# A list scheduler with its own lengths for each group of images, and spare products on TensorE

## The chip, the cores and the metric

The kernel runs on one core of one Trainium2 chip. The metric is the time on the device in microseconds (us) of one execution, lower being better. Its engines work side by side: TensorE (PE, matrix products), VectorE (DVE), ScalarE (ACT), GpSimd (POOL), and SyncE (SP), which only issues DMA transfers here.

## The reference

The network is one vision block on 32 images of 96 x 96 pixels, 36 patches of an image being its tokens (1152 tokens, 192 features):

```
h = patches(x) @ W.T + b                       # 768 -> 192
h = h + mamba(layernorm(h))                    # in-projection and gate (192 -> 384), a selective scan
                                               # over the 36 tokens with 16 states, out-projection, FFN of 512
h = h + moe(layernorm(h))                      # router, 16 experts (192 -> 2 x 192 -> 192), top 4 of 16
```

In the scan each of 384 channels has 16 states: `h[t] = a_bar[t] * h[t-1] + dt*z*B[t]`, and `y[t] = sum over states of h[t] * C[t]`. The step size `dt` is a softplus of a projection. The experts are computed for all tokens and weighted with the router's result. Everything is float32.

## The kernel before, in words

The images are cut into five groups, called cuts, of 4, 7, 7, 7 and 7 images (144 and 252 tokens). For each cut the work is a long list of steps, each a few instructions, and each step has a part on one or two engines:

- *Before the scan*: six embed parts, mean, variance, `roots` (VectorE) and `power` (GpSimd) for the norm, `spread` (TensorE puts the root on all partitions), `scale` (VectorE), three in-projections with gate, a projection to the inputs of the scan (`xproj`, `dt_in`, `bc_copy`), `delta` with its copies on ScalarE (`delta_abs`), the softplus as a product of factors (`factor`, `poly`, `log1p`), and `drive` (on VectorE in cut 0, on GpSimd in the others).
- *C spreads*: eight times `c_spread` (TensorE) and `c_copy` (ScalarE) put C on all partitions. In the kernel the first `c_spread` of a cut waits for `bc_low` and for the copies of `delta` (lines 861 to 871).
- *Scan*: 24 steps of `decay` (ScalarE), `fill` (TensorE), `drive_b` and `advance` (VectorE, the recurrence), `read` (GpSimd) and `collect` (TensorE).
- *After the scan*: out-projection, norm, the FFN (`ffn_up`, `ffn_tanh`, `ffn_product`, `down`), and the next norm.
- *Experts*: the router (`x_logits`, `x_topk`, `x_exp`, `x_route`, `x_turn`, `x_mix`), `x_start`, then 24 units of `x_gate`, `x_linear`, work on VectorE, ScalarE and GpSimd, and `x_down`. `x_start` opens the sums in the PSUM bank `sums`.
- *Splitting* the first expert weights in two parts, `split_w1`, sixteen steps on ScalarE and GpSimd with loads from DRAM, once at the start.

All engines follow one order, written by `schedule()` (line 234) before the program is built: `run` (line 610) lets each engine go through this order and issue what is its own. Semaphores see to correctness, so the order settles only which work stands before which on each engine.

`schedule()` is a list scheduler on the host. It holds five streams: the steps before the scan with the C spreads of cuts 0, 2, 3 and 4; those of cut 1; the scans; the work after the scans; the experts; with `split_w1` as a further one. A stream is a list of turns (a turn is one to a few steps), and each turn has a place, in units of scan steps, at which it is due. Again and again it takes, of the turns at the streams' heads whose needs are met, the one with the lowest

```
score = place + WAIT_WEIGHT * waits
```

`waits` is the time for which TensorE and VectorE would stand idle for this turn. `lay` (line 250) works it out: it lays the turn's steps on the engines' own times, with durations from the table `COST` (line 341) scaled as `0.25 + 0.75 * size` where size is the cut's tokens over 252. A step starts when its engine is free and its inputs are ready. For scan and expert steps the inputs are listed (`rests_on`, line 220); for every other step they are the ends of the steps before it in its turn, and for a turn's first step the end of the stream's turn before. So the planner starts a cut's first `c_spread` after its `drive`.

Of the kernel before, what the change touches and what calls it, by code (L numbers as in the profile page):

```python
# [20 lines left out]
P = 128  # L21
# [23 lines left out]
NC = len(CUTS)  # L45
# [188 lines left out]
def schedule():  # L234

    out, given, ended = [], set(), {}  # L240
    free = {"P": 4.0, "V": 4.0, "S": 10.0, "G": 4.0}
    streams, reading = [], [0.0]

    def stream(turns, places):
        streams.append(list(zip(turns, places)))

    def spread_over(n, first, last):
        return [first + (last - first) * k / max(1, n - 1) for k in range(n)]

    def lay(turn, chain, keep):  # L250

        at, waits, end, pool_from = dict(free), 0.0, {}, reading[0]
        for c, step, i in turn:
            size = TOKENS[c] / TM
            ready = chain
            found = rests_on(c, step, i)
            if found is not None:
                ready = max([end.get((c, *f), ended.get((c, *f), 0.0)) for f in found])
            elif end:
                ready = max(ready, max(end.values()))  # L260
            for engine, us in COST[step]:
                start = max(at[engine], ready)
                if step in TWO_PORTS and pool_from <= start:
                    start = max(start, at["G"])
                if engine in "PV":
                    waits += start - at[engine]
                elif engine == "G":
                    pool_from = start
                at[engine] = start + us * (0.25 + 0.75 * size)
                ready = at[engine] + LATENCY[engine]  # L270
            end[(c, step, i)] = ready
        if keep:
            free.update(at)
            reading[0] = pool_from
            ended.update(end)
        return waits, max(end.values())

    prep = []
    for c in range(NC):
        b, s = of_cut(c, before_scan()), of_cut(c, c_turns())  # L280
        if c == 0:
            places = spread_over(len(b), -24.0, -1.0) + spread_over(len(s), -1.0, 5.0)
        elif c == 1:
            places = spread_over(len(b), -16.0, 20.0) + spread_over(len(s), 17.0, 24.0)
        else:
            p = SCAN_STEPS * (c - 1)
            places = spread_over(len(b), p, p + BEFORE_SPAN) + spread_over(len(s), p + 17.0, p + 24.0)
        if c == 1:
            stream(b + s, places)
        else:  # L290
            prep += list(zip(b + s, places))
    streams.append(prep)
    scans = []
    for c in range(NC):
        turns = scan_turns(c)
        if c:
            ends = of_cut(c - 1, scan_end(c - 1))
            turns = of_cut(c, turns)
            first = turns.index([(c, "collect", 0)])
            turns = turns[:first - 2] + ends + turns[first - 2:]  # L300
        else:
            turns = of_cut(0, turns)
        scans += list(zip(turns, spread_over(len(turns), SCAN_STEPS * c, SCAN_STEPS * (c + 1) - 0.4)))
    scans += [(turn, SCAN_STEPS * NC) for turn in of_cut(NC - 1, scan_end(NC - 1))]
    streams.append(scans)
    posts, routed = [], []
    for c in range(NC):
        a, x = of_cut(c, after_scan()), of_cut(c, expert_turns())
        p = SCAN_STEPS * (c + 1) + 2.0
        q = p + (AFTER_SPAN if c + 2 < NC else LAST_AFTER_SPAN)  # L310
        posts += list(zip(a, spread_over(len(a), p, q)))
        routed += list(zip(x, spread_over(len(x), q + 0.5, q + (EXPERT_SPAN if c + 2 < NC else LAST_EXPERT_SPAN))))
    streams += [posts, routed]
    stream([[(0, "split_w1", n)] for n in range(2 * PAIRS)], [-12.0, -8.0, -5.0, -2.0] + spread_over(12, *SPLIT_SPAN))
    chain = [0.0] * len(streams)

    while any(streams):
        best = None
        for n, turns in enumerate(streams):
            if not turns:  # L320
                continue
            turn, place = turns[0]
            inside = {s for s in turn}
            if any(f not in given and f not in inside for step in turn for f in needed(*step)):
                continue
            waits, end = lay(turn, chain[n], False)
            score = place + WAIT_WEIGHT * waits
            if best is None or score < best[0]:
                best = (score, n)
        assert best, [t[0] for t in streams if t]  # L330
        n = best[1]
        turn, _ = streams[n].pop(0)
        _, end = lay(turn, chain[n], True)
        chain[n] = end
        out += turn
        given.update(turn)
    return out
# [2 lines left out]

COST = {
    "embed": (("P", .87),), "embedded": (("S", .9),), "mean": (("P", .85),), "center": (("V", .6),),
    "square": (("S", .56),), "variance": (("P", .9),), "roots": (("V", .18),), "power": (("G", 1.),),
    "spread": (("P", .45),), "scale": (("V", 1.5),), "inproj": (("P", 1.7),),
    "gate": (("S", .32),), "z": (("V", .38),), "xproj": (("P", 1.27),), "dt_in": (("S", .45),),
    "bc_copy": (("V", .36),), "bc_high": (("S", .36),), "bc_low": (("V", .4),), "delta": (("P", .65),),
    "delta_abs": (("S", 1.2),), "delta_exp": (("S", .75),), "factor": (("S", .9),),
    "poly": (("V", .7),), "log1p": (("V", .72),), "drive": (("G", 2.2),), "c_spread": (("P", .25),),
    "c_copy": (("S", .52),), "decay": (("S", .82),), "fill": (("P", .25),), "drive_b": (("V", .6),),
    "advance": (("V", 1.13),), "read": (("G", 1.2),), "collect": (("P", .85),), "y": (("V", .43),),  # L350
    "outproj": (("P", 1.27),), "y1_add": (("V", .6),), "square2": (("S", .62),), "variance2": (("P", .9),),
    "roots2": (("V", .18),), "power2": (("G", 1.),), "spread2": (("P", .23),),
    "scale2": (("V", .78),), "ffn_up": (("P", 1.7),), "ffn_tanh": (("S", .36),), "ffn_product": (("V", .78),),
    "down": (("P", 1.7),), "h1": (("V", .55), ("G", 1.25)), "mean3": (("P", .85),), "center3": (("V", .58),),
    "square3": (("S", .62),), "variance3": (("P", .9),), "roots3": (("V", .18),), "power3": (("G", 1.),),
    "spread3": (("P", .45),), "scale3": (("V", 1.5), ("G", 1.3)),
    "t_high": (("S", .62),), "t_low": (("G", 1.25),), "x_logits": (("P", .9),), "x_topk": (("V", 2.2),),
    "x_exp": (("S", .3),), "x_route": (("V", 1.2),), "x_turn": (("P", .25),), "x_mix": (("S", .7),),
    "x_start": (("P", .85),), "x_gate": (("P", .6),), "x_linear": (("P", .6),), "x_min": (("V", .43),),
    "x_tanh": (("S", .33),), "x_one": (("S", .4),), "x_low": (("V", .41),), "x_gated": (("V", .34),),  # L360
    "x_glu": (("G", .68),), "x_scale": (("G", .68),), "x_down": (("P", .47),), "x_finish": (("V", 1.2),),
    "split_w1": (("S", 1.), ("G", 2.)),
}

TWO_PORTS = {"x_gated", "poly", "log1p", "bc_low"}

LATENCY = {"P": 0.22, "V": 0.12, "S": 0.1, "G": 0.14}
WAIT_WEIGHT = 0.5
BEFORE_SPAN = 15.5
AFTER_SPAN, LAST_AFTER_SPAN = 20.9, 22.0  # L370
EXPERT_SPAN, LAST_EXPERT_SPAN = 25.1, 21.7
SPLIT_SPAN = (2.0, 36.0)


def vit_tower(nc, patches, embed_w, in_w, in_w_rest, xproj_w, dt_w, out_w, ffn_w, ffn_w_rest,
# [5 lines left out]
    with ExitStack() as ctx:  # L381
# [10 lines left out]
        w_embed = sb("w_embed", [P, KP, 2 * P])  # L392
# [14 lines left out]
        decay = sb("decay", [P, NJ, STATES])  # L407
# [8 lines left out]
        at, first = {}, 0  # L416
# [13 lines left out]
        us = sb("us", [P, 2, NJ, TM])  # L430
# [9 lines left out]
        dt_in = sb("dt_in", [DT_RANK, TM])  # L440
# [326 lines left out]
        def _(pe):  # L767
            def mm(out, lhsT, rhs, start, stop, shared=False, turned=False):

                return nc.tensor.matmul(out, lhsT, rhs, start=start, stop=stop, skip_group_check=shared,  # L770
                                        is_transpose=turned)

            def embed(c, part):
# [236 lines left out]
            def x_down(c, n):  # L1010
# [9 lines left out]
                else:  # L1020
# [5 lines left out]
            run({"embed": embed, "mean": mean, "variance": variance, "spread": spread, "inproj": inproj,  # L1026
                 "xproj": xproj, "delta": delta, "c_spread": c_spread, "fill": fill, "collect": collect,
                 "outproj": outproj, "variance2": variance2, "spread2": spread2, "ffn_up": ffn_up, "down": down,
                 "mean3": mean3, "variance3": variance3, "spread3": spread3, "x_logits": x_logits,
# [578 lines left out]
```

## Time and profile before

| what | value |
|---|---|
| median of 3 runs | 625.59 us (624.6 to 626.37) |
| the profiled execution | 627.44 us, span 625.6 us |
| mean granted clock of TensorE | 0.945 |
| TensorE, weight loads busy | 557.0 us, 479.1 us |
| VectorE, GpSimd, ScalarE busy | 475.5 us, 388.3 us, 295.2 us |

The span goes from the first to the last instruction; the execution's own time lies around it. Busy time is per engine, and engines overlap. The granted clock is TensorE's own: 1.0 is 2.4 GHz and 0.5 is 1.2 GHz, and these are its only two levels in the records, so a mean between them is a mixture in time. Nearly all TensorE instructions have one line, 770, that of the helper `mm`; they are told apart by their tiles: `pre` and `post` are PSUM banks of the work before and after the scan (cut 1 is prepared in `post`), `fills` and `y_sum` those of the scan, `gate_up`, `linear_up` and `sums` those of the experts.

### The profile page before, as it was taken

Reading aid. Unit: us, or ns where it says so; the run is one execution under the profiler, and the core shown is the slowest. Engines: PE = TensorE matmul, PEld = TensorE weight load, DVE = VectorE, ACT = ScalarE, POOL = GpSimd, SP = SyncE. Lnnn points to the kernel's source line nnn. Section 1 sums busy time; section 2 is a strip of 40 time slices with the busy share of each in tenths; the row PEclk is TensorE's granted clock in tenths of the full one; section 3 lists DMA queues with packets and bytes.
Section 4 is the critical chain, followed back from the end, with each engine's and each line's share of the span. In section 5 each row is a group of like instructions: output and inputs, shape, how many; then the busy total and the mean of one; then the engine's idle time right before and its main releaser. Section 6 shows DMA issues by size and latency. Waiting matters only on the chain.

```text
span 625.6 us, 10398 instructions
## 1 busy us (share of the span) xinstructions
PE 557.0 (89%) x3361; PEld 479.1 (77%) x3361; DVE 475.5 (76%) x897; ACT 295.2 (47%) x699; POOL 388.3 (62%) x447
## 2 busy tenths in 40 slices
PE   3959589977899999989999997999998889978896
PEld 3748478866698988879887885988886768857785
DVE  1166868889789789979879996999989556565664
ACT  1167846483544475544446474445442324323442
POOL 3257777767456458857555984767677355564674
PEclk9779959989899999999999997999999889997999
DMA  9993533432053343413343341554342266553781
GB/s 238 308 299 97 164 119 90 189 135 92 1 155 100 106 155 95 162 33 112 111 171 112 105 141 46 135 157 143 121 177 88 50 207 213 178 174 104 238 274 52
DMA packets 41827, 88.34 MB, mean 141 GB/s; under 512 B 9581, under 2 KB 34477, under 8 KB 35501
## 3 DMA queue, kind: packets, MB, share of 16 engines
q1 hardware_dynamic: 41772, 87.68, 43.4%
q8 instruction: 26, 0.43, 0.3%
q14 instruction: 29, 0.23, 0.1%
HBM read 77.24 MB, written 10.40 MB: 140 GB/s over the span
## 4 chain that ended last, share of the span: by engine, by line
PE 61%; DVE 15%; issue 6%; DMA 6%; ACT 5%; POOL 4%; SPq 2%; POOLq 0%; DVEq 0%; ACTq 0%
PE post L770 12%; PE y_sum L770 10%; PE sums L770 10%; PE gate_up L770 10%; PE pre L770 8%; PE linear_up L770 8%; DVE state L1255 4%; DMA w<-w_store 3%; PE fills L770 3%; DVE fills L1246 2%; DVE dts L1222 2%; SPq L709 1%; POOL read L1456 1%; DMA hid<-patches 1%; DVE scratch L1354 1%
## 5 line engine op out<-in xcount | busy, mean ns | idle before, releaser
L1456 POOL TENSOR_TENSOR read<-state,c_all 128x504 f32<-128x504 f32 (+1 forms) x120 | 147.0, 1228 | 83.2 <-DVE state L1255 54.8
L1255 DVE TENSOR_TENSOR_SCAN state<-a_bar,fills 128x504 f32<-128x504 f32 (+1 forms) x120 | 133.0, 1109 | 12.1 <-ACT a_bar L1035 4.1
L1485 POOL TENSOR_TENSOR scratch<-scratch 128x252 f32<-128x252 f32 (+1 forms) x120 | 81.6, 680 | 87.4 <-DVE scratch L1369 82.4
L770 PE MATMUL y_sum<-read,ident 128*128 128x252 f32 (+1 forms) x480 | 122.5, 382 | 4.1 <-POOL read L1456 3.7
L1035 ACT ACTIVATE scratch<-scratch 128x252 f32<-128x252 f32 (+1 forms) x120 | 47.3, 394 | 147.0 <-DVE scratch L1354 146.8
L770 PE MATMUL sums<-hid,w 128*128 128x252 f32 (+1 forms) x480 | 103.8, 377 | 4.8 <-POOL hid L1494 4.8
L770 PE MATMUL gate_up<-t_high,w 128*128 128x252 f32 (+1 forms) x360 | 89.3, 318 | 14.5 <-DVE route L1332 7.2
L770 PEld LDWEIGHTS y_sum<-read,ident 128*128 128x128 f32 x480 | 86.3, 201 | 19.8 <-issue 7.1
L1035 ACT ACTIVATE a_bar<-dts,decay 128x245 f32<-128x245 f32 (+1 forms) x240 | 100.2, 470 | 2.2 <-DVE dts L1230 2.2
L1494 POOL TENSOR_TENSOR hid<-scratch,route_rows 128x252 f32<-128x252 f32 (+1 forms) x120 | 84.9, 708 | 14.4 <-DMA route_rows<-mix_rows 7.6
L770 PE MATMUL linear_up<-t_high,w 128*128 128x252 f32 (+1 forms) x360 | 85.8, 308 | 2.3 <-ACT mix_w L1035 1.7
L770 PEld LDWEIGHTS gate_up<-t_high,w 128*128 128x128 f32 x360 | 64.3, 193 | 27.8 <-issue 17.0
L1354 DVE TENSOR_SCALAR scratch<-gate_up,vec 128x252 f32<-128x252 f32 (+1 forms) x120 | 54.0, 450 | 40.0 <-PE gate_up L770 39.1
L1246 DVE TENSOR_TENSOR fills<-us,fills 128x504 f32<-128x504 f32 (+1 forms) x120 | 75.6, 630 | 7.8 <-PE fills L770 7.6
L1369 DVE SCALAR_TENSOR_TENSOR scratch<-scratch 128x252 f32<-128x252 f32 (+1 forms) x120 | 76.1, 634 | 4.4 <-POOL scratch L1485 0.3
L1361 DVE TENSOR_SCALAR scratch<-linear_up,vec 128x252 f32<-128x252 f32 (+1 forms) x120 | 54.2, 451 | 22.1 <-PE linear_up L770 19.1
L770 PEld LDWEIGHTS linear_up<-t_high,w 128*128 128x128 f32 x360 | 63.8, 193 | 6.6 <-ACT mix_w L1035 2.7
L770 PE MATMUL fills<-bc_parts,pick_state 128*128 128x252 f32 (+1 forms) x240 | 60.6, 336 | 8.0 <-DVE state L1255 8.0
L770 PE MATMUL gate_up<-t_low,w 128*128 128x252 f32 (+1 forms) x240 | 62.0, 282 | 0.0
L770 PE MATMUL linear_up<-t_low,w 128*128 128x252 f32 (+1 forms) x240 | 61.8, 281 | 0.0
L770 PEld LDWEIGHTS sums<-hid,w 128*128 128x128 f32 x480 | 49.0, 163 | 15.9 <-POOL hid L1494 6.6
L1035 ACT ACTIVATE scratch<-scratch,ones 128x252 f32<-128x252 f32 (+1 forms) x120 | 58.5, 488 | 4.3 <-POOL scratch L1485 0.5
(166 smaller groups left out, 851.9 us busy)
## 6 DMA issues: line engine op xcount, KB each, us to landing
w<-w_store SPq DMA_DIRECT2D x40, 1152.0 KB, 5.7
route_rows<-mix_rows SPq DMA_DIRECT2D x192, 63.0 KB, 3.0
w_store<-w SPq DMA_DIRECT2D x8, 1152.0 KB, 5.0
scratch<-expert_w SPq DMA_DIRECT2D x16, 384.0 KB, 5.6
w<-expert_w SPq DMA_DIRECT2D x1, 2304.0 KB
route_rows<-mix_rows SPq DMA_DIRECT2D x48, 36.0 KB, 2.8
w_embed<-embed_w SPq DMA_DIRECT2D x3, 256.0 KB, 3.9
x_patch<-patches SPq DMA_DIRECT2D x1, 756.0 KB, 5.0
```

Of the source, the lines that this page charges most:

```text
L709: sp.dma_start(route_rows[part * REST:(part + 1) * REST, slot, 0:tok(c)], mix_rows[c % 2][e:e + 1, 0:tok(c)].to_broadcast([REST, tok(c)]))\
L770: return nc.tensor.matmul(out, lhsT, rhs, start=start, stop=stop, skip_group_check=shared, is_transpose=turned)
L1035: return nc.scalar.activation(out, in_, func, **kw)
L1222: dve.scalar_tensor_tensor(dt, factors[:, k % FACTOR_SLOTS, :, 0:tok(c)], LOG1P[k][1], dt if k else sp_exp[:, :, 0:tok(c)], ALU.add, ALU.m ...
L1246: dve.tensor_tensor(b_x, twice(us[:, c % 2, j, 0:tok(c)]), b_x, ALU.mult).then_inc(bx_ready.sem, 1)
L1255: dve.tensor_tensor_scan(pair(state, i, c), pair(a_bar, i, c), pair(fills, i, c), 0.0, ALU.mult, ALU.add).then_inc(scanned.sem, 1)
L1354: dve.tensor_scalar(g_min[un % 2][:, 0:tok(c)], half(gate_up, c, 0), col("b1_gate", un), LIMIT, ALU.add, ALU.min).then_inc(gate_min.sem, 1)
L1361: dve.tensor_scalar(l_min[:, 0:tok(c)], half(linear_up, c, 0), col("b1_linear", un), 1.0 + LIMIT, ALU.add, ALU.min).then_inc(linear_min.se ...
L1369: dve.scalar_tensor_tensor(product[un % 2][:, 0:tok(c)], l_min[:, 0:tok(c)], 1.0 - LIMIT, g_min[un % 2][:, 0:tok(c)], ALU.max, ALU.mult).t ...
L1456: pool.tensor_tensor(by_state(pair(read, i, c)), by_state(pair(state, i, c)), c_all[:, n:n + 2, 0:tok(c)], ALU.mult).then_inc(read_out.sem, 1)
L1485: pool.tensor_tensor(glu[:, 0:tok(c)], product[un % 2][:, 0:tok(c)], g_one[un % 2][:, 0:tok(c)], ALU.mult)\
L1494: pool.tensor_tensor(hid[:, un % HID_TILES, 0:tok(c)], glu[:, 0:tok(c)], route_rows[:, slot, 0:tok(c)], ALU.mult).then_inc(hid_ready.sem, 1)
```

## The change

Two things change, both in `schedule()`, and one helper is added on TensorE.

The planner's numbers: some durations in `COST`, mostly of ScalarE, are set anew; the fixed share of a step's duration is now its engine's own (`FIXED`) instead of 0.25; `WAIT_WEIGHT` goes from 0.5 to 1.5; the lengths over which the places of a group are spread are given for each cut and stream (for cuts 0 and 1 those of `BEFORE_SPANS` are not read, as their places are given elsewhere).

Spare products: `lay` also notes the longest idle time of TensorE within the turn (`idle`). Before a turn with 0.8 us or more of it, as long as the first `x_start` hasn't been given, the order gets `(idle - 0.2) / 0.24` steps `warm`, and ten more stand before cut 1's first embed part. A `warm` step multiplies a 128 x 128 tile of the embed weights with itself into the bank `sums`, waits for nothing and signals nothing; its result is never read.

```
     def lay(turn, chain, keep):
...
+                if engine == "P":
+                    idle[0] = max(idle[0], start - at["P"])
...
-                at[engine] = start + us * (0.25 + 0.75 * size)
+                at[engine] = start + us * (FIXED[engine] + (1.0 - FIXED[engine]) * size)
...
-            places = spread_over(len(b), p, p + BEFORE_SPAN) + spread_over(len(s), p + 17.0, p + 24.0)
+            places = spread_over(len(b), p, p + BEFORE_SPANS[c]) + spread_over(len(s), p + 17.0, p + 24.0)
...
-        q = p + (AFTER_SPAN if c + 2 < NC else LAST_AFTER_SPAN)
+        q = p + AFTER_SPANS[c]
...
-        routed += list(zip(x, spread_over(len(x), q + 0.5, q + (EXPERT_SPAN if c + 2 < NC else LAST_EXPERT_SPAN))))
+        routed += list(zip(x, spread_over(len(x), q + 0.5, q + EXPERT_SPANS[c])))
...
+        if (0, "x_start", 0) not in given and idle[0] >= WARM_FROM:
+            out += [(0, "warm", k) for k in range(int((idle[0] - WARM_MARGIN) / WARM_STEP))]
+        out += [(0, "warm", k) for k in range(WARM_AT.get(turn[0], 0))]
         out += turn
...
-    "poly": (("V", .7),), "log1p": (("V", .72),),
+    "poly": (("V", 0.9),), "log1p": (("V", 0.85),),
...
+FIXED = {"P": 0.08, "V": 0.22, "S": 0.5, "G": 0.22}
-WAIT_WEIGHT = 0.5
-BEFORE_SPAN = 15.5
-AFTER_SPAN, LAST_AFTER_SPAN = 20.9, 22.0
-EXPERT_SPAN, LAST_EXPERT_SPAN = 25.1, 21.7
+WAIT_WEIGHT = 1.5
+BEFORE_SPANS = (39.85, 11.8, 19.57, 15.32, 14.59)
+AFTER_SPANS = (23.32, 20.9, 19.43, 21.5, 24.02)
+EXPERT_SPANS = (22.68, 25.68, 25.23, 23.04, 21.62)
+WARM_FROM, WARM_MARGIN, WARM_STEP = 0.8, 0.2, 0.24
+WARM_AT = {(1, "embed", 0): 10}
...
+            def warm(_, k):
+                mm(sums[:, 0:P], w_embed[:, 0, 0:P], w_embed[:, 0, 0:P], True, True)
```

Besides `poly` and `log1p`, fourteen other durations move by 0.01 to 0.06 us.

## Rows read from the trace of the kernel before

**Rows 1.** The page: TensorE's busy time, and its granted clock in 40 slices (tenths)
```profile
PE 557.0 (89%) x3361; PEld 479.1 (77%) x3361; DVE 475.5 (76%) x897; ACT 295.2 (47%) x699; POOL 388.3 (62%) x447
...
PEclk9779959989899999999999997999999889997999
```

**Rows 2.** The page: the chain that ended last, by engine
```profile
PE 61%; DVE 15%; issue 6%; DMA 6%; ACT 5%; POOL 4%; SPq 2%; POOLq 0%; DVEq 0%; ACTq 0%
```

**Rows 3.** Windows by stage: length; busy PE, PEld, DVE, ACT, POOL; clock; DMA share, GB/s
```profile
0.00:170.00 170.00, 130.44 (x680) 112.06 (x681) 114.27 (x197) 92.49 (x229) 103.05 (x112) 0.87 0.49 159
170.00:480.00 310.00, 300.37 (x1888) 262.98 (x1888) 274.38 (x493) 152.75 (x360) 206.86 (x232) 0.99 0.38 122
480.00:625.60 145.60, 126.15 (x796) 104.03 (x794) 86.88 (x208) 49.95 (x110) 78.39 (x104) 0.94 0.50 161
```

**Rows 4.** Windows at low clock
```profile
14.70:24.40 9.70, 8.77 (x33) 7.52 (x34) 1.23 (x5) 0.00 (x0) 3.24 (x4) 0.50 1.08 335
...
76.00:93.00 17.00, 13.94 (x52) 12.20 (x52) 11.94 (x18) 8.82 (x22) 14.11 (x15) 0.50 0.37 116
...
380.00:390.00 10.00, 6.52 (x26) 5.57 (x27) 7.09 (x22) 5.27 (x14) 4.31 (x4) 0.66 0.04 10
```

**Rows 5.** Timeline, 15 to 26 us: start, length, engine, line, what, [idle before <-releaser]
```profile
15.63 2.05 PE L770 MATMUL post<-hid,w_embed 128*128 128x252 f32 x4 [3.33 <-DMA hid<-patches]
...
17.48 0.33 PE L770 MATMUL pre<-mean_ones,squares 128*72 128x1 f32 x2
...
18.39 2.03 PE L770 MATMUL post<-hid,w_embed 128*128 128x252 f32 x4
...
18.88 1.04 POOL L1406 TENSOR_TENSOR roots<-roots,minus_half 72x4 f32<-72x4 f32 x1 [3.10 <-DVE roots L1186]
...
20.21 0.69 PE L770 MATMUL pre<-ident,roots 72*128 72x72 f32 x4
...
21.58 0.36 DVE L1196 SCALAR_TENSOR_TENSOR squares<-centered,vec,pre 128x144 f32<-128x144 f32 x1
...
22.46 0.69 PE L770 MATMUL pre<-squares,w_in 128*128 128x144 f32 x2
...
24.38 1.21 PE L770 MATMUL post<-hid,w_embed 128*128 128x252 f32 x4
...
25.43 0.41 PE L770 MATMUL pre<-squares,w_in 128*128 128x144 f32 x2
...
25.67 0.41 PE L770 MATMUL pre<-squares,w_in_rest 128*128 128x144 f32 x2
```

**Rows 6.** Timeline of TensorE: the first and the longest of its early waits
```profile
11.46 0.48 PE L770 MATMUL pre<-h0s,mean_ones 128*128 128x144 f32 x2 [2.20 <-ACT h0s L1035]
...
41.30 1.10 PE L770 MATMUL post<-ident,roots 126*128 126x126 f32 x4 [4.91 <-POOL roots L1406]
```

**Rows 7.** Timeline: the drives (us<-dts) and first C spreads (bc_parts,pick_state), cuts 0, 1
```profile
41.80 0.61 DVE L1237 TENSOR_TENSOR us<-dts,zs 128x432 f32<-128x432 f32 x1
...
42.05 0.68 PE L770 MATMUL pre<-bc_parts,pick_state 128*128 128x144 f32 x2
...
82.84 0.80 PE L770 MATMUL post<-bc_parts,pick_state 128*128 128x252 f32 x2
...
85.48 1.78 POOL L1444 TENSOR_TENSOR us<-dts,zs 128x756 f32<-128x756 f32 x1
```

**Rows 8.** The chain in order of time: start, length, what
```profile
44.32 3.74 PE post L770 x8
...
77.02 1.33 PE y_sum L770 x4
...
87.44 0.81 PE post L770 x2
...
139.35 1.83 DVE dts L1222
...
164.48 3.48 PE pre L770 x8
```

More of the change, by code:

```diff
@@ L241, in schedule @@
     free = {"P": 4.0, "V": 4.0, "S": 10.0, "G": 4.0}
-    streams, reading = [], [0.0]
+    streams, reading, idle = [], [0.0], [0.0]
     def stream(turns, places):
@@ L252, in lay @@
         at, waits, end, pool_from = dict(free), 0.0, {}, reading[0]
+        idle[0] = 0.0
         for c, step, i in turn:
@@ L342 @@
     "embed": (("P", .87),), "embedded": (("S", .9),), "mean": (("P", .85),), "center": (("V", .6),),
-    "square": (("S", .56),), "variance": (("P", .9),), "roots": (("V", .18),), "power": (("G", 1.),),
+    "square": (("S", 0.61),), "variance": (("P", .9),), "roots": (("V", .18),), "power": (("G", 1.),),
     "spread": (("P", .45),), "scale": (("V", 1.5),), "inproj": (("P", 1.7),),
-    "gate": (("S", .32),), "z": (("V", .38),), "xproj": (("P", 1.27),), "dt_in": (("S", .45),),
+    "gate": (("S", 0.37),), "z": (("V", .38),), "xproj": (("P", 1.27),), "dt_in": (("S", .45),),
     "bc_copy": (("V", .36),), "bc_high": (("S", .36),), "bc_low": (("V", .4),), "delta": (("P", .65),),
     "delta_abs": (("S", 1.2),), "delta_exp": (("S", .75),), "factor": (("S", .9),),
[L348 to L351, printed above, removed]
+    "poly": (("V", 0.9),), "log1p": (("V", 0.85),), "drive": (("G", 2.2),), "c_spread": (("P", .25),),
+    "c_copy": (("S", 0.57),), "decay": (("S", 0.8),), "fill": (("P", .25),), "drive_b": (("V", 0.62),),
+    "advance": (("V", 1.15),), "read": (("G", 1.26),), "collect": (("P", .85),), "y": (("V", .43),),
+    "outproj": (("P", 1.27),), "y1_add": (("V", .6),), "square2": (("S", 0.62),), "variance2": (("P", .9),),
     "roots2": (("V", .18),), "power2": (("G", 1.),), "spread2": (("P", .23),),
-    "scale2": (("V", .78),), "ffn_up": (("P", 1.7),), "ffn_tanh": (("S", .36),), "ffn_product": (("V", .78),),
+    "scale2": (("V", .78),), "ffn_up": (("P", 1.7),), "ffn_tanh": (("S", 0.37),), "ffn_product": (("V", .78),),
     "down": (("P", 1.7),), "h1": (("V", .55), ("G", 1.25)), "mean3": (("P", .85),), "center3": (("V", .58),),
@@ L358 @@
     "x_exp": (("S", .3),), "x_route": (("V", 1.2),), "x_turn": (("P", .25),), "x_mix": (("S", .7),),
-    "x_start": (("P", .85),), "x_gate": (("P", .6),), "x_linear": (("P", .6),), "x_min": (("V", .43),),
-    "x_tanh": (("S", .33),), "x_one": (("S", .4),), "x_low": (("V", .41),), "x_gated": (("V", .34),),
-    "x_glu": (("G", .68),), "x_scale": (("G", .68),), "x_down": (("P", .47),), "x_finish": (("V", 1.2),),
+    "x_start": (("P", .85),), "x_gate": (("P", .6),), "x_linear": (("P", .6),), "x_min": (("V", 0.44),),
+    "x_tanh": (("S", 0.38),), "x_one": (("S", 0.45),), "x_low": (("V", 0.43),), "x_gated": (("V", .34),),
+    "x_glu": (("G", 0.7),), "x_scale": (("G", 0.71),), "x_down": (("P", .47),), "x_finish": (("V", 1.2),),
     "split_w1": (("S", 1.), ("G", 2.)),
@@ L1024, in x_down @@
                     last.then_inc(pe_hid.sem, 1)
-            run({"embed": embed, "mean": mean, "variance": variance, "spread": spread, "inproj": inproj,
+            run({"warm": warm, "embed": embed, "mean": mean, "variance": variance, "spread": spread, "inproj": inproj,
                  "xproj": xproj, "delta": delta, "c_spread": c_spread, "fill": fill, "collect": collect,
```

## The prediction

> **What bounds the kernel now.** I read the busy times first. TensorE is the busiest engine: 557 us of a 625.6 us span, and the row of granted clock under it is far from flat [rows 1]. Next I read the chain that ended last: 61% of it is TensorE, 15% VectorE, 4% GpSimd [rows 2]. Then I cut the span by stage. From 170 to 480 us TensorE is busy for 300.4 of 310 us at a mean clock of 0.99, so there it is simply full. Before 170 us it is busy for 130.4 of 170 us at a mean clock of 0.87: both idle and slow. After 480 us it is busy for 126.2 of 145.6 us at 0.94 [rows 3].
>
> A mean clock of 0.87 over 170 us, with only the two levels 1.0 and 0.5, is 2 x 0.13 x 170 = 44 us at half speed. They come in blocks: 14.7 to 24.4 us, and 76 to 93 us, where TensorE was busy for 13.9 of 17 us at half clock [rows 4]; between them one near 38 to 48 us, and short ones near 138 and 165 us. Each follows a stretch in which TensorE had stood still: the first comes after the wait of 3.33 us for the patches of cut 1 [rows 5].
>
> A block costs only what of it lies on the path, so it has to be walked. In the first, the path is on TensorE from 15.63 us: an embed part (to 17.48), the variance (to 18.39), a root on VectorE and GpSimd (to 19.92), the spread (from 20.21, since an embed part stood before it), the scale on VectorE (to 21.94), the first in-projection (22.46 to 24.38) [rows 5].
>
> **The change, part by part.** The time is summed against the profiled execution, 627.44 us with a span of 625.6; it lies 0.3% above the median of 625.59, so I take the difference from 625.6.
>
> *What a spare tile costs.* It is one 128 x 128 by 128-column product in f32, two matmul instructions. The same with 144 columns takes 25.67 - 25.43 = 0.245 us at full clock and 0.48 us at half (four of them from 22.46 to 24.38) [rows 5]. By columns, 128/144 of it: 0.22 us, or 0.43 at half clock. Tiles wait for nothing, so they start when TensorE's queue reaches them. They are free as long as the wait that follows is longer than they are, and otherwise the rest delays every matmul behind them.
>
> *How many.* The ten before cut 1's first embed part take 2.2 us, inside its 3.33 us wait for a transfer that they can't lengthen [rows 5]. For the others the planner's own idle time decides. Twelve waits of at least 0.8 us stand in the trace before the first expert start, 25 us together; the first is 2.20 us, the longest 4.91 us [rows 6]. At (wait - 0.2)/0.24 each, without the transfer that the planner doesn't see, they ask for about 75 tiles. The planner sees two more that the kernel doesn't have. It lets the first C spread of a cut begin when its stream's last turn, the drive, has ended. In the trace cut 0's C spread starts at 42.05 us while the drive runs to 42.41, and cut 1's at 82.84 us, 2.6 us before its drive even begins [rows 7]. It listens only to the projection's copies. If the planner sees 2 to 5 us there, each spread gets 8 to 20 tiles that no real wait covers: 1.8 to 4.4 us each. So 100 to 130 tiles in all, 22 to 29 us of TensorE time, against 39.6 us of idle TensorE before 170 us [rows 3].
>
> *What a kept clock gives back.* First block: the embed part 0.93, the variance 0.45, the spread's delay behind an embed part 0.29 and its own half 0.24, the in-projection's delay 0.52 and half 0.96: 3.4 us [rows 5]. Second block: 3.74 us of in-projection on the chain at 44.32 us, half of it 1.9 us. Third block: ten TensorE pieces of the chain between 77.02 and 88.25 us add up to 8.6 us; half is 4.3 us, but VectorE and GpSimd are busy for 11.9 and 14.1 of these 17 us [rows 4] and come next, so it is between 0 and 4.3 and I take 3. Near 139 us the chain is on VectorE, so the down-projection's slowness gives nothing. At 164.48 us 3.48 us of embed on the chain give 1.7 us [rows 8]. Sum: 3.4 + 1.9 + 3 + 0 + 1.7 = 10 us.
>
> *What misplaced tiles take.* The two C spreads, 3.6 to 8.8 us together. Behind the one at 42 us stand cut 1's in-projection and the third fill of the scan, behind the one at 82 us the copies of C and the last fills of cut 0. VectorE has work of its own at both places, so part of it is covered: I take 3.5 us. Were the clock low there all the same, a tile would be 0.43 us and the two would take up to 17 us. Tiles elsewhere may overrun by a few tenths; I leave them in the range.
>
> *The new order.* Tripling the weight of a wait makes the planner prefer a turn that starts at once on TensorE or VectorE to one that is due. The per-engine fixed shares shorten cut 0's TensorE steps and lengthen its ScalarE ones, since only cut 0 is shorter; the spans move turns by a few scan steps (those of cuts 0 and 1 in the list for the steps before the scan are read nowhere, as both cuts have places of their own). No instruction is added by this. TensorE has 9.6 us of idle time from 170 to 480 us [rows 3], and one slow place in it, 380 to 390 us, with 6.5 us busy at a clock of 0.66 [rows 4]; the planner itself can't win more than these 12 us there. A bad order can lose as much: a recurrence pushed back holds the fills. Between -12 and +12 I take 0, since the stage is 97% full already. The waits after 480 us belong to the last cuts, which have little to put between, and get no tiles.
>
> The Trainium skill ("TensorE: Matmul & The Clock Gate", Part 1, on the two states) says the ramp penalty is under 1% of a typical kernel's span. By that the whole clock gain would be an estimate of under 6.3 us and, with my misplaced tiles, the change under 3 us. The rows speak against it here: 44 us at half clock before 170 us, in five blocks and not one ramp.
>
> Sum: -10 + 3.5 + 0 = -6.5 us. After 170 us TensorE is full, so what is won before it moves the end by the same. 625.6 - 6.5 = **619.1 us**, 1.0% less.
>
> **Rivals.**
>
> *More comes back* (602 to 614 us). The misplaced tiles lie beside VectorE's work, all of the third block returns (10 + 1.3 = 11.3 us), and the new order wins a few of the 12 us. For it: TensorE is only 77% busy before 170 us. Against it: ScalarE, VectorE and GpSimd bound the third block. At the middle: 610.
>
> *The tiles don't hold the clock, or what they win is lost at once* (623.7 to 627.5 us). The planner places by its own times; where a real wait outlasts the tiles, as at 41.30 us, the clock may fall behind them. Then they lie in idle time and change nothing. For it: planned and real waits differ by transfers and by GpSimd's splitting of the weights. Against it: it has to fail in all of the first three blocks.
>
> *Misplaced tiles decide* (slower). Mechanism: the C spreads' wait exists in the planner alone. If both get 20 tiles and the clock there is low, it takes 17 us against 10 - 3 = 7 us from what other blocks give back: +10, 636 us. At full clock and without the third block it takes 8.8 against 7: +1.8, 627.4 us. It decides from 32 such tiles at full clock, or 16 at half. For it: both spreads start in the trace without the planned wait. Against it: the heavier weight on waits makes the planner put other turns there first, and fewer tiles follow.
>
> *The order alone loses* (slower, about 630 us). The scan's turns are passed over for turns that start at once, VectorE's recurrences come late, and half of the 12 us in the full stage goes on top of a small early gain. Nothing in the trace tells its sign.
>
> **How the numbers follow.** About 0.3% (1.9 us) is what a measurement can tell from no change here. Chances: forecast (614 to 623.7) 0.44, more comes back 0.20, nothing 0.13, misplaced tiles 0.12, order 0.11. Faster is the first two, 0.64; same 0.13; slower 0.23. The forecast's own range is 614 to 623.7; leaving a tenth out at each end gives 606 to 631.
>
> **What would show it.** Right: granted clock near 1.0 from 14 to 24 us, cut 0's first in-projection ending near 21 us instead of 24.4, and the first expert start some 6 us earlier, with all later stages moved by the same. The misplaced tiles show as a run of some ten spare products directly before the first C spread of cuts 0 and 1, with VectorE or ScalarE waiting for it. The prediction is wrong if the early stage gains over 10 us, if it gains nothing with the clock high, or if 170 to 480 us changes its length by over 5 us: then the order, not the tiles, made the difference.

## The result: 2.45% slower

The changed kernel takes 641.18 us (median of 4 runs, 638.82 to 642.47), the one before 625.98 us on the same chip. The ratio is 1.0245, 95% interval 1.0214 to 1.0276: 15 us slower, where 6.5 us less were forecast and the range ended at 631.

The page of the changed kernel: TensorE's busy time and its granted clock in 40 slices, and the chain that ended last.

```profile
PE 579.6 (91%) x3655; PEld 505.5 (79%) x3655; DVE 470.8 (74%) x897; ACT 295.3 (46%) x699; POOL 388.7 (61%) x447
...
PEclk9899999799999999989999997999999799998899
...
PE 63%; DVE 9%; DMA 8%; POOL 7%; issue 6%; ACT 4%; SPq 3%; POOLq 0%; DVEq 0%; ACTq 0%
```

147 spare products were placed, some 34 us at 0.23 us each; TensorE's busy time grows by only 22.6 us [rows 1]: its other products take less time, as more of them run at the full clock. On the chain VectorE's share falls from 15% to 9%, DMA's rises from 6% to 8% and GpSimd's from 4% to 7% [rows 2].

The stages of the changed kernel (length; busy TensorE, weight loads, VectorE, ScalarE, GpSimd; clock; DMA share, GB/s):

```profile
0.00:170.00 170.00, 143.94 (x941) 131.90 (x941) 107.70 (x176) 88.73 (x218) 100.10 (x109) 0.96 0.48 159
170.00:480.00 310.00, 298.39 (x1874) 261.96 (x1873) 267.18 (x502) 154.24 (x366) 202.67 (x228) 0.98 0.37 118
480.00:639.70 159.70, 137.24 (x844) 111.68 (x842) 95.92 (x221) 52.30 (x116) 85.90 (x112) 0.94 0.47 155
```

The clock of the first 170 us is 0.96 where it was 0.87 [rows 3]: over the stage the tiles do what they are for. In its first block they do so only in part, 0.82 where it was 0.50 [rows 4]:

```profile
14.70:24.40 9.70, 5.92 (x28) 5.17 (x29) 0.22 (x2) 2.36 (x6) 4.88 (x6) 0.82 0.42 129
```

But VectorE gets 107.7 us of work done in that stage instead of 114.3. So the clock was kept for the most part and the work fell behind all the same. A few marks, read from the timelines of the profiled executions (us from the start), show where:

| mark | before | changed | difference |
|---|---|---|---|
| step sizes of cut 0 (`log1p` starts) | 41.2 | 44.2 | +3.0 |
| step sizes of cut 1 | 84.0 | 81.3 | -2.7 |
| step sizes of cut 2 | 141.3 | 157.8 | +16.5 |
| first expert start, cut 0 | 173.2 | 186.8 | +13.6 |
| result of cut 0 | 264.9 | 272.6 | +7.7 |
| result of cut 2 | 479.4 | 487.2 | +7.8 |
| expert start, cut 3 | 490.9 | 504.5 | +13.6 |
| result of cut 4 | 622.0 | 636.0 | +14.0 |

Two places stand out. In the first 170 us the kernel falls behind; 13.6 us are missing at the first expert start, and 7.8 of them still at cut 2's result. And the 11.5 us between cut 2's result and cut 3's expert start have become 17.2.

**The first place.** Timeline of ScalarE and TensorE in the changed kernel (start, length, engine, line, what, [idle before <-releaser]):

```profile
12.21 2.40 PE L784 MATMUL sums<-w_embed 128*128 128x128 f32 x20
...
15.86 1.98 ACT L1053 ACTIVATE w<-scratch 128x384 fp32r<-128x384 f32 x4 [4.47 <-DMA scratch<-expert_w]
...
17.75 0.43 ACT L1053 ACTIVATE squares<-centered 128x288 f32<-128x288 f32 x1
...
18.08 0.25 ACT L1053 ACTIVATE read<-post 48x128 f32<-48x128 f32 x1
...
18.48 3.62 PE L784 MATMUL post<-hid,w_embed 128*128 128x252 f32 x8 [3.87 <-ACT read L1053]
...
22.61 0.23 PE L784 MATMUL pre<-mean_ones,squares 128*72 128x1 f32 x2
...
26.48 0.48 PE L784 MATMUL pre<-squares,w_in 128*128 128x144 f32 x2 [0.25 <-DVE squares L1214]
```

The tiles end at 14.6 us and the patches of cut 1 were there near 15.6 us in the kernel before [rows 5]. But the first embed part now waits for ScalarE's `read` (the exponential of the decay, which the kernel wants done before it writes the bank `post`), and that stands behind two steps of `split_w1`, which wait 4.47 us for raw expert weights to arrive. In the kernel before, ScalarE squared at 12.82 us and split at 24.82:

```profile
12.82 0.44 ACT L1035 ACTIVATE squares<-centered 128x288 f32<-128x288 f32 x1 [1.50 <-DVE centered L1178]
...
24.82 0.93 ACT L1035 ACTIVATE w<-scratch 128x384 fp32r<-128x384 f32 x2
```

The variance of cut 0 moves from 17.48 to 22.61 us and its first in-projection from 22.46 to 26.48. The Trainium skill ("TensorE: Matmul & The Clock Gate", Part 1, "Architectural detail") calls ScalarE's queue strictly first in, first out; the trace agrees: the square's input was ready at 12.9 us, when VectorE's centering ended, and the square starts at 17.75 us, behind the splits.

It happens again with cut 2:

```profile
115.73 0.94 ACT L1053 ACTIVATE w<-scratch 128x384 fp32r<-128x384 f32 x2 [4.32 <-DMA scratch<-expert_w]
```

```profile
117.23 0.38 PE L784 MATMUL pre<-mean_ones,squares 128*126 128x1 f32 x2 [3.59 <-ACT squares L1053]
...
118.75 2.03 PE L784 MATMUL y_sum<-read,ident 128*128 128x252 f32 x4
```

ScalarE waits 4.32 us for raw weights, cut 2's variance on TensorE waits 3.59 us for the square behind it, and the next products run at half clock (2.03 us for four that take 1.01 at full clock).

**The second place.** TensorE of the changed kernel after cut 2's result:

```profile
493.78 0.76 PE L784 MATMUL gate_up<-t_high,w 128*128 128x252 f32 x2 [3.17 <-DVE route L1350]
...
494.98 1.89 PE L784 MATMUL y_sum<-read,ident 128*128 128x252 f32 x4
497.53 5.38 PE L784 MATMUL post<-y,w_out 128*128 128x252 f32 x12 [0.66 <-DVE y L1278]
502.70 0.62 PE L984 MATMUL linear_up<-ident,route 126*16 126x126 f32 x2
...
504.47 1.01 PE L784 MATMUL sums<-mix_w,b 128*128 128x252 f32 x4
```

TensorE waits 3.17 us for the router of cut 3, comes back at half clock, and does the whole out-projection of cut 4 (5.38 us) before the router's transpose, on which the expert start depends. In the order before, half of the out-projection stood there and half behind:

```profile
484.81 0.47 PE L770 MATMUL gate_up<-t_high,w 128*128 128x252 f32 x2 [1.98 <-DVE route L1332]
...
485.47 2.62 PE L770 MATMUL post<-y,w_out 128*128 128x252 f32 x6
487.88 0.63 PE L966 MATMUL linear_up<-ident,route 126*16 126x126 f32 x2
...
489.66 1.44 PE L770 MATMUL post<-y,w_out 128*128 128x252 f32 x6
490.93 1.01 PE L770 MATMUL sums<-mix_w,b 128*128 128x252 f32 x4
```

**The misplaced tiles.** Of the 147 tiles 32 stand before C spreads: 15 before the first of cut 0, 12 before the first of cut 2, none before the first of cut 1. Both of these runs are on the chain of the changed kernel (here without the part of each that runs under other work):

```profile
45.02 3.35 PE sums L784 x30
...
157.99 2.79 PE sums L784 x24
```

### The profile page after: what moved, and what is told of

Its sections match the earlier page's. It is cut to its first block, busy times and chain, and to the rows that moved or that the text cites. A ratio compares the mean times of both kernels' runs of the same rounds, so it can differ in the third digit from the quotient of the medians.

```text
span 639.7 us, 10986 instructions
## 1 busy us (share of the span) xinstructions
PE 579.6 (91%) x3655; PEld 505.5 (79%) x3655; DVE 470.8 (74%) x897; ACT 295.3 (46%) x699; POOL 388.7 (61%) x447
## 4 chain that ended last, share of the span: by engine, by line
PE 63%; DVE 9%; DMA 8%; POOL 7%; issue 6%; ACT 4%; SPq 3%; POOLq 0%; DVEq 0%; ACTq 0%
PE post L784 13%; PE y_sum L784 11%; PE sums L784 11%; PE gate_up L784 9%; PE pre L784 9%; PE linear_up L784 7%; DMA w<-w_store 3%; DMA scratch<-expert_w 3%; PE fills L784 3%; DVE state L1273 2%; POOL read L1474 2%; POOL hid L1512 1%; DVE fills L1264 1%; SPq L723 1%; POOL scratch L1503 1%
## 5 line engine op out<-in xcount | busy, mean ns | idle before, releaser
L1474 POOL TENSOR_TENSOR read<-state,c_all 128x504 f32<-128x504 f32 (+1 forms) x120 | 144.9, 1212 | 83.4 <-DVE state L1273 52.1
L1503 POOL TENSOR_TENSOR scratch<-scratch 128x252 f32<-128x252 f32 (+1 forms) x120 | 83.7, 698 | 89.5 <-DVE scratch L1387 80.2
L1387 DVE SCALAR_TENSOR_TENSOR scratch<-scratch 128x252 f32<-128x252 f32 (+1 forms) x120 | 68.7, 573 | 4.2
L784 PEld LDWEIGHTS sums<-hid,w 128*128 128x128 f32 x480 | 49.0, 163 | 15.6 <-POOL hid L1512 6.2
```

The source lines that it names most:

```text
L1387: dve.scalar_tensor_tensor(product[un % 2][:, 0:tok(c)], l_min[:, 0:tok(c)], 1.0 - LIMIT, g_min[un % 2][:, 0:tok(c)], ALU.max, ALU.mult).t ...
L1474: pool.tensor_tensor(by_state(pair(read, i, c)), by_state(pair(state, i, c)), c_all[:, n:n + 2, 0:tok(c)], ALU.mult).then_inc(read_out.sem, 1)
L1503: pool.tensor_tensor(glu[:, 0:tok(c)], product[un % 2][:, 0:tok(c)], g_one[un % 2][:, 0:tok(c)], ALU.mult)\
```

## Experiments

Ratios are against the kernel before, run beside each. Where a difference of two versions is given, it is the difference of their ratios, times 626 us; by the two intervals it is known to 2 to 3 us either way (an estimate).

**Without tiles (`no_tiles`).**
```
-            out += [(0, "warm", k) for k in range(int((idle[0] - WARM_MARGIN) / WARM_STEP))]
+            pass
-WARM_AT = {(1, "embed", 0): 10}
+WARM_AT = {}
```


> The changed kernel without its spare products (all 147 left out), same order otherwise. Theory W (the new order makes ScalarE wait for the raw expert weights, and that costs the 14 us): the time stays above 635 us, and with a low clock in the first 50 us it may reach 645. Rival T (the spare products stand in TensorE's way): 622 to 630 us.

644.76 us, 1.0292 (1.0251 to 1.0333). The order alone costs 18 us. The tiles give 3 of them back by the difference (1.0292 against 1.0245), but the two intervals overlap, so that gain is not clear of noise. That the tiles are what loses is out for the new order.

**Tiles alone (`before_tiles`).** The old planner, with the rule for spare products and `warm` as the only addition.

> The kernel before with the spare products alone: its old planner, numbers and order, and 148 tiles put in by the new rule. Theory W: the tiles by themselves are no loss, 615 to 627 us. Rival T: they alone bring most of the loss, 633 to 642 us.

632.51 us, 1.0098 (1.0068 to 1.0127): between the two. With the old order the tiles lose 6.1 us. TensorE of this run around the two C spreads:

```profile
40.01 0.65 PE L779 MATMUL post<-ident,roots 126*128 126x126 f32 x4 [3.45 <-POOL roots L1418]
40.49 4.70 PE L779 MATMUL sums<-w_embed 128*128 128x128 f32 x26
44.94 0.42 PE L779 MATMUL pre<-bc_parts,pick_state 128*128 128x144 f32 x2
```

```profile
83.35 4.18 PE L779 MATMUL sums<-w_embed 128*128 128x128 f32 x36
87.29 0.48 PE L779 MATMUL post<-bc_parts,pick_state 128*128 128x252 f32 x2
```

4.7 and 4.2 us of tiles stand before the first C spreads of cuts 0 and 1, with no idle time behind either, and both are on this run's chain. In the kernel before, these C spreads came at 42.05 and 82.84 us [rows 7]; here they come at 44.94 and 87.29.

**Splits held back (`pinned`).** Each split may be placed only after the step that it followed in the order before (the fourteenth: after cut 2's square). The planner then also lays some other steps a few places earlier or later, so this run changes more than the splits.
```
+    if step == "split_w1" and i in SPLIT_AFTER:
+        return [SPLIT_AFTER[i]]
...
+SPLIT_AFTER = {0: (0, 'gate', 0), 1: (1, 'embedded', 0), 2: (0, 'bc_high', 0), ...
```


> The changed kernel, with each of the 16 steps that split the raw expert weights held back in the planner until the step that it followed in the order before (for the fourteenth: until cut 2's square). Theory W: the waits of ScalarE for raw weights near 16, 39 and 116 us go, cut 0's variance comes near 17 us again instead of 22.6, and the time falls by 8 to 14 us, to 626 to 632. Rival T, or a rival O (the later order of scans and experts loses the time): no more than 3 us come back, 636 to 642.

637.15 us, 1.0178 (1.0153 to 1.0202). 4 us come back, half or less of what theory W asked for. Its step sizes of cut 0 start at 38.3 us and its cut 2 result at 479.6, level with before (479.4); the 17 us up to cut 3's expert start remain, and so does a later end.

**Two splits early, nothing else (`before_split_early`).**
```
+    early = [(0, "split_w1", 0), (0, "split_w1", 1)]
+    out = [step for step in out if step not in early]
+    at_center = out.index((0, "center", 0))
+    return out[:at_center] + early + out[at_center:]
```


> The kernel before, with only the first two steps that split the raw expert weights moved ahead of cut 0's centering and square, as in the changed kernel; no tiles. Theory W: cut 0's variance moves from 17.5 to about 22.5 us and the whole kernel is 3 to 5 us longer, 629 to 631. Rivals T and O: what cut 0 loses there is covered by the waits behind it, within 1.5 us of 625.6.

630.04 us, 1.0067 (1.0042 to 1.0093): 4.2 us, the price of the early splits by themselves, as theory W had it. Every other step keeps its place in this run. ScalarE's wait and what stands behind it are those of the changed kernel:

```profile
16.49 1.99 ACT L1038 ACTIVATE w<-scratch 128x384 fp32r<-128x384 f32 x4 [5.48 <-DMA scratch<-expert_w]
...
18.72 0.26 ACT L1038 ACTIVATE read<-post 48x128 f32<-48x128 f32 x1
...
20.93 0.33 PE L773 MATMUL pre<-mean_ones,squares 128*72 128x1 f32 x2
...
25.92 0.69 PE L773 MATMUL pre<-squares,w_in 128*128 128x144 f32 x2
```

Two steps of 1 us each, moved forward by 8 and 14 us (from 24.82 and 31.19 us) on a queue of an engine that is busy for half of the time, cost 4 us at the end.

**Tiles alone, none before C spreads (`tiles_no_spread`).**
```
-        if (0, "x_start", 0) not in given and idle[0] >= WARM_FROM:
+        if (0, "x_start", 0) not in given and idle[0] >= WARM_FROM and turn[0][1] != "c_spread":
```


> The kernel before with the spare products alone, without the 35 of them that stand before C spreads (113 stay). Theory M (the tiles that cost are those before C spreads, where only the planner waits): 4 to 8 us less than with all 148, so 624 to 628. Rival A (every tile costs, by lying in front of work whose real wait differs from the planned one): the loss falls with the number only, 35/148 of 6.6 us, to 630 to 632.

623.99 us, 0.9960 (0.9934 to 0.9986): the misplaced tiles (those before C spreads) are what loses in the old order. These 35 tiles before C spreads cost 8.6 us in the old order; the other 113 gain 2.5. This version beats both kernels, by a little. Its chain shows why the gain is small:

```profile
14.76 1.12 PE post L779 x4
...
19.42 1.22 PE pre L779 x8
...
26.78 7.54 DMA scratch<-expert_w
34.34 0.94 ACT w L1047 x2
```

Cut 0's first in-projection starts at 19.42 us instead of 22.46 [rows 5], 3.0 us earlier; 0.9 of that is the patches of cut 1, on which the embed part waits in both and which came at 14.76 instead of 15.63 us. Then a load of raw weights, 7.54 us, lets ScalarE's next split start only at 34.34 us, after 1.70 us of idle time, and cut 0's step sizes come at 39.02 instead of 41.16. SyncE issues that load behind TensorE's last embed part of cut 1, so a faster TensorE does move its start, here and before:

```profile
26.78 1.71 SPq L685 DMA_DIRECT2D scratch<-expert_w x1
```

```profile
30.81 0.65 SPq L676 DMA_DIRECT2D scratch<-expert_w x1
```

What it doesn't shorten is the load itself. Issued 4.0 us earlier, the load took 7.54 us; in the kernel before it had landed when ScalarE came to it at 36.50 us, 5.7 us after its issue.

**The planner's numbers one by one (`weight15`, `spans`, `durations`).** Each time the kernel before with only `WAIT_WEIGHT = 1.5`; or only the new lists of spans; or only the new `FIXED`; no tiles. The run `durations` leaves the table `COST` as it was, though its expectation speaks of new durations, so no run has the new `COST` as its only change; and in that table `poly` and `log1p` move by 0.20 and 0.13 us, not by hundredths.

> The kernel before with WAIT_WEIGHT 1.5 as the only change, no tiles. Theory V (the weight is what makes the new order slow: it puts the first two splits of raw weights ahead of cut 0's centering, and turns that wait for nothing ahead of those that are due): 635 to 645 us, most of the 18.8 us that the new order loses. Rival S (the spans or durations do it): 628 to 631, the 4 us of the early splits and no more.

> The kernel before with the new lengths for each cut and stream as the only change, no tiles. Theory V: within 3 us of 626. Rival S: 632 to 640, with the loss between the end of cut 2 and the expert start of cut 3.

> The kernel before with the new durations and fixed shares as the only change, no tiles. Theory V: within 3 us of 626, since the shares move cut 0 alone and the durations by hundredths. Rival S: over 630.

The weight: 636.11 us, 1.0173 (1.0119 to 1.0228). The spans: 634.06 us, 1.0113 (1.0059 to 1.0168), in four runs from 628.78 to 637.06. The fixed shares: 627.23 us, 1.0021 (0.9999 to 1.0043), no change that can be told. Together 1.7 + 1.1 + 0.2 = 3.0%, against 2.9% in `no_tiles` for these three and `COST`. If parts added, nothing would be left for `COST`; further down they don't always add, so what `COST` does stays open. Both theories were half right: the weight is the larger part, the spans are one too. Rival S looked for the spans' loss between the end of cut 2 and the expert start of cut 3; the profiled execution of `spans`, the fastest of the four, has 13.8 us there against 11.5, and its first expert start is 5.3 us late. The weight alone already puts the first two splits ahead of cut 0's centering.

**The weight with the splits held back (`weight15_pinned`).** `WAIT_WEIGHT = 1.5` and `SPLIT_AFTER` in the kernel before.

> The kernel before with WAIT_WEIGHT 1.5 alone and the 16 splitting steps held back as in the run pinned; no tiles. Theory V1 (the weight loses its time by drawing the splits forward): of the 10.2 us that the weight costs 7 or more come back, 626 to 629. Theory V2 (it loses as much by the order of the scans and experts after that): 4 us come back, as from pinned, 630 to 634.

639.11 us, 1.0196 (1.0163 to 1.0229): neither. Nothing came back. Cut 0's step sizes are at 40.7 us again (45.3 in `weight15`), yet the result of cut 2 is at 490.8 (before 479.4). TensorE's longest wait of this run and the same wait before, from the views of waits (us in total, times, longest):

```profile
PE fills L774 <- DVE state L1259: 16.6, 11, 5.8
```

```profile
PE fills L770 <- DVE state L1255: 8.0, 7, 2.1
```

The scan's fills wait twice as long for the recurrence. But in `weight15` itself that wait is 7.9 us, as before, so the longer wait belongs to the order that the planner makes with the splits held back, and not to the weight alone. What the run shows is that holding the splits back is no cure by itself: with the old spans it gains nothing, with the new ones 4 us.

**Which tiles gain (`tiles_first45`, `ten_only`, `ten_and_late`).** Tiles alone, none before C spreads: those up to cut 1's spread (45); the ten of `WARM_AT`; those ten and the 68 behind cut 1's spread (78).

> The kernel before with the spare products alone, only those up to cut 1's spread (45 tiles, the first 40 us) and none before a C spread. Theory E (what tiles give is the clock of the first two blocks, 2 us or so): 622 to 625, the same as with 113 tiles. Rival L (the later 68 tiles keep the clock of the third block and give more than they take): 625 to 627.

> The kernel before with only the ten tiles ahead of cut 1's first embed part. Theory E: they keep the clock of the first block; the first in-projection comes 2 to 2.5 us earlier, but the load of raw weights that ScalarE then waits for takes half of it back: 624 to 625.5. Rival L: no more than 0.5 us, 625.5 to 627.

> The kernel before with 78 spare products: the ten ahead of cut 1's first embed part and those behind cut 1's spread, none before C spreads. Theory E2 (the ten give 1.8 us, the 68 later ones another 1.7, the 35 between them take back 1.8): 621 to 623. Rival N (what is won in the first 170 us beyond 2 us is lost again in the full stage, whatever the tiles): 623.5 to 625.5.

625.69 us, 0.9998 (0.9977 to 1.0018); 623.88 us, 0.9974 (0.9958 to 0.9991); 624.92 us, 0.9975 (0.9954 to 0.9997). `tiles_first45` falls in rival L's range, `ten_only` just below theory E's, `ten_and_late` in rival N's. By the medians the ten tiles before the wait for a transfer give nearly all that tiles give, but all four intervals (with `tiles_no_spread`) lie between 0.993 and 1.002 and overlap, and the parts don't add. What fits best is that no part of the tiles matters much: beyond some 2 us nothing of what a kept clock wins early is found again at the end.

**Fewer tiles in the new order (`pinned_no_spread`).** The run `pinned` without tiles before C spreads.

> The changed kernel with the splits held back as in pinned and without the tiles before C spreads (105 of 151 stay). If the two causes found add up: 637.2 less about 6 to 8 us, 629 to 631, still slower than before by what spans and weight lose later. If the tiles cost nothing in this order (taking all out made it slower): 635 to 638.

637.77 us, 1.0197 (1.0163 to 1.0231), `pinned` being 1.0178: no gain. What cost 8.6 us in the old order costs nothing in this one. The changed kernel itself was not run without them.

**The router's transpose first (`turn_first`, `pinned_turn_first`).** Cut 4's out-projection moves behind cut 3's expert start; once in the changed kernel, once in `pinned`.
```
+    late = [(4, "outproj", 0), (4, "outproj", 1)]
+    out = [step for step in out if step not in late]
+    at_start = out.index((3, "x_start", 0)) + 1
+    return out[:at_start] + late + out[at_start:]
```


> The changed kernel with the out-projection of cut 4 moved behind cut 3's router transpose and first expert start, everything else as it is. Theory G (the 5.8 us lost between the end of cut 2 and that expert start come from the out-projection, 5.4 us at half clock, standing before the router's transpose): 636 to 638.5 us, the expert start near 499 instead of 504.5. Rival H (the last cut is late in any case and the transposition only changes who waits): 639.5 to 643.

> The same move in the run pinned (splits held back as before, all tiles). Theory G: the two causes add, 637.2 less 3 to 5 us, 632 to 634.5. Rival H: 636 to 639.

636.97 us, 1.0170 (1.0145 to 1.0195), and 631.79 us, 1.0073 (1.0047 to 1.0100). The out-projection's place costs 4.7 and 6.6 us. TensorE of `turn_first` (this view ends at 503 us, before the last of twelve matmuls):

```profile
495.20 0.76 PE L787 MATMUL gate_up<-t_high,w 128*128 128x252 f32 x2 [3.17 <-DVE route L1353]
...
496.40 1.89 PE L787 MATMUL y_sum<-read,ident 128*128 128x252 f32 x4
498.08 0.58 PE L987 MATMUL linear_up<-ident,route 126*16 126x126 f32 x2
...
499.82 1.01 PE L787 MATMUL sums<-mix_w,b 128*128 128x252 f32 x4
500.66 2.50 PE L787 MATMUL post<-y,w_out 128*128 128x252 f32 x11
```

The transpose follows the half-clock product directly; expert start 11.2 us after cut 2's result instead of 17.2, and the out-projection, behind it, runs at full clock. Together the two moves take the loss from 2.45% to 0.73%.

**What is left (`old_spans`, `old_spans_no_spread`, `pinned_turn_no_spread`).** The changed kernel with the old spans; that with the splits held back and no tiles before C spreads; `pinned_turn_first` without tiles before C spreads.

> The changed kernel with the spans of before (weight, durations and spare products by the new rule stay). If weight, spans and durations add, as their single runs do (10.2, 8.1 and 1.3 us for 18.8 together): 641.2 - 8, 631 to 635, and the 5.8 us between the end of cut 2 and cut 3's expert start are gone. If the spans do harm only alone: 638 to 643.

> The run old_spans with the splits held back and without the spare products before C spreads. If the causes add: 633.5 less 4 for the splits and less some for the tiles, 624 to 629. If holding back the splits does nothing with these spans, as with the weight alone: 631 to 635.

> The run pinned_turn_first without the spare products before C spreads (105 of 151 stay). If those still stand in TensorE's way there, as with the old order (8.6 us): 625 to 629, no longer slower than before. If the new order covers them, as leaving them out of pinned suggested (637.2 and 637.8): 630 to 634.

633.49 us, 1.0107 (1.0088 to 1.0125): the spans' share is really in the changed kernel, 8.6 us of its 15, and with the old spans cut 3's expert start comes 11.7 us after cut 2's result. Yet here too all of cut 4's out-projection stands before the router's transpose:

```profile
488.30 0.76 PE L784 MATMUL gate_up<-t_high,w 128*128 128x252 f32 x2 [2.10 <-DVE route L1350]
...
489.50 3.78 PE L784 MATMUL post<-y,w_out 128*128 128x252 f32 x12
493.12 0.38 PE L984 MATMUL linear_up<-ident,route 126*16 126x126 f32 x2
```

`weight15` has the same order there and 11.8 us, while `spans` has half before and half behind. So the weight puts the out-projection in front, and that place costs little as long as the spans are old. With the new ones the last product of cut 4's scan (`y_sum`, 494.98 us) and a wait for VectorE's `y` stand there as well, the router takes longer, and more runs at half clock; which of these makes the price was not tested apart.

628.29 us, 1.0056 (1.0030 to 1.0083): with splits and tiles set right too, 0.6% are left for weight, `COST` and `FIXED`. 635.21 us, 1.0157 (1.0122 to 1.0193), above the ranges of both: here leaving those tiles out costs 5 us (1.0157 against 1.0073); the clock from 120 to 170 us falls from 0.99 to 0.88. Against `pinned_no_spread` (1.0197) this run also gives a third price for the out-projection's place, 2.5 us, which is not clear of noise.

## Why the prediction was wrong, step by step

*That the tiles keep the clock* was right for the stage: 0.96 for 0.87 before 170 us. The rival that they don't hold it is out. The sign named for the first block failed in the changed kernel: near 1.0 was expected from 14 to 24 us and 0.82 measured, since behind the ten tiles TensorE waits another 3.87 us for ScalarE; cut 0's first in-projection, expected to end near 21 us, starts at 26.48.

*What a kept clock gives back*, 10 us, was four times too large. In the old order 113 tiles gave 2.5 us. The first block's term was about right where it was read: from the first embed part to the end of the first in-projection 8.75 us became 5.72, 3.0 us less (3.4 forecast). It was wrong at the end: with the patches 0.9 us early besides, 3.9 us were won there and 2.1 left at cut 0's step sizes, since behind it stands a load that a faster TensorE starts earlier but doesn't shorten. I added up blocks as if the path behind each were TensorE's.

*How many tiles* was low: 147 and some 34 us, where 100 to 130 and 22 to 29 us were forecast. Behind the first load thirteen waits of at least 0.8 us, 25.8 us in all, stand in the kernel before, not twelve.

*Misplaced tiles*, taken at 3.5 us with 8.8 as the upper bound, cost 8.6 us in the old order, the bound itself: little or nothing covered them. The mechanism was the one predicted, a wait that exists in the planner alone. In the changed kernel's order they stand before cuts 0 and 2 and not, as forecast, before cuts 0 and 1; with the splits held back they cost nothing or even help. The term has no fixed size.

*The new order*, taken at 0 within 12 us, is the step that made the sign wrong: alone it costs 18 us. The bound was read from idle TensorE between 170 and 480 us, as if the order could only lose there. From the first expert start to cut 2's result the changed kernel is in fact 5.9 us shorter (300.4 us against 306.3). It lost before that, in part through a queue that I had not looked at, and again after 480 us, which I had passed over. The spans, taken as moves by a few scan steps with no price, cost 7 us alone. I had the weight prefer turns that start at once on TensorE or VectorE and left out those that use neither. `waits` counts TensorE and VectorE only, so a turn of `split_w1` (ScalarE and GpSimd) never has any; a heavier weight makes every turn that waits dearer and this one never. It went ahead, on an engine that works in order, into a wait for a transfer that the planner doesn't know. The rival that the order alone loses had the sign and 0.11, but another mechanism and 630 us.

The Trainium skill's under 1% for the clock's ramp ("TensorE: Matmul & The Clock Gate", Part 1), against which I argued with 44 us at half clock, was the better guide to what comes back: the tiles are worth 0.4% in the old order without the misplaced ones and, against `no_tiles`, 0.5% in the new one, the latter not clear of noise.

*What is shown and what isn't.* Shown by doing it alone: the two early splits, 4 us; holding all splits back gives the same 4 us in the changed kernel, but nothing with the weight alone. Shown by moving it, twice: the place of the out-projection before cut 3's router, 5 to 7 us with all tiles; not clear of noise without those before C spreads. Shown by single changes: weight and spans lose, the fixed shares don't. Not tested: the new `COST`. Not settled: how the weight loses the rest, what the spans add at the out-projection, and what they lose elsewhere.

## What to carry to other kernels

A list scheduler's score speaks only for the engines in it: before its weight is raised, list the steps that the score can't see, for they may move first, as here, and on an in-order engine a step that waits for a transfer holds all behind it. Time at half clock is not by itself time to be won; follow the path behind the block to the next transfer, whose length a faster TensorE leaves as it is. Filler work belongs before waits that the trace shows, as the ten tiles before a known transfer, and not before waits that a planner computes.

## What was not expected of the hardware

A spare product costs what was estimated (22 of them in 5.12 us, 0.23 us each, at 37.45 us), and up to twice that where the tiles themselves ran at low clock: 0.36 us in `before_tiles` (13 in 4.70 us, granted clock 0.61), 0.40 in `ten_only` (10 in 4.03 us, granted clock 0.55) and 0.44 in `ten_and_late` (10 in 4.41 us), by its length half clock, for which 0.43 was estimated. So in the last two the ten tiles outlasted the 3.33 us by which they were to be covered; the embed part behind them waits for nothing more and runs at full clock (1.02 us for what took 2.05 in the kernel before). Small shifts in the first 170 us come out at the end with either sign: among the four versions of tiles with the old order, cut 0's first expert start, in one profiled execution each, lies between 168.4 and 172.3 us, and the medians between 623.9 and 625.7 don't follow it.
